# A fused attention and mixture-of-experts kernel: the fourth block's attention moved to the end, expert 0 moved between two blocks

## The reference, cut to what matters

```python
x  = inputs                        # (B=4, S=512, D=128), so 2048 tokens
xn = (x - mean(x)) / sqrt(var(x) + 1e-5)
# attention over each batch row
y = xn @ U                                        # U (128, 32)
attn = softmax(-(n_t + n_j - 2 y_t . y_j))        # n = sum(y*y)
att = attn @ xn
# mixture of 8 experts, two for each token, and a shared expert
xf = xn.reshape(2048, 128)
probs = softmax(rmsnorm(xf) @ router_w.T);  topk_p, topk_i = top_k(probs, 2)
# expert e takes the first 320 of its tokens, in token order
xg = xf[dispatch]                                 # (8, 320, 128)
eout = (silu(xg @ rg) * (xg @ ru)) @ rd           # 8 x (128->512->128)
routed[dispatch] += eout * weight_of_token
shared = (silu(xn @ sg) * (xn @ su)) @ sd         # 128->1024->128
out = x + att + shared + routed
```

## Time and profile before

| what | us |
|---|---|
| median of 3 runs | 156.9 (156.74 to 157.12) |
| the profiled execution, time | 156.88 |
| the profiled execution, span | 155.4 |
| TensorE busy | 150.5 (97% of the span) |
| TensorE weight load busy | 135.1 (87%) |
| VectorE busy | 117.4 (76%) |
| ScalarE busy | 103.5 (67%) |
| GpSimd busy | 83.2 (54%) |

### The profile page before, as it was taken

How to read it: one execution, slowest core, us unless ns; L and a number is a source line. 1 busy time by engine, 2 the same in 40 slices (tenths; PEclk the granted TensorE clock), 3 DMA queues, 4 the chain that set the end, 5 groups by cost and what they waited for, 6 DMA issues and landing times.

```text
span 155.4 us, 3117 instructions
## 1 busy us (share of the span) xinstructions
PE 150.5 (97%) x964; PEld 135.1 (87%) x964; DVE 117.4 (76%) x290; ACT 103.5 (67%) x217; POOL 83.2 (54%) x102
## 2 busy tenths in 40 slices
PE   6999999999999999999999999999999999999992
PEld 6878777889999888888888899999999999878991
DVE  3999969899735599998988777786786786546871
ACT  3369999999469397768756569889677466334100
POOL 7653422357777787877400005698988847454000
PEclk9999999999999999999999999999999999999999
DMA  4999999981111117435069300423232011118486
GB/s 128 302 275 111 210 308 343 343 245 54 55 53 51 51 54 218 158 80 172 0 173 259 124 0 2 152 58 98 67 103 72 25 46 34 30 32 291 96 273 186
DMA packets 26638, 20.72 MB, mean 133 GB/s; under 512 B 2333, under 2 KB 22840, under 8 KB 26624
## 3 DMA queue, kind: packets, MB, share of 16 engines
q1 hardware_dynamic: 24544, 17.76, 42.4%
q0 software_dynamic: 1792, 2.65, 5.6%
q10 hardware_dynamic: 288, 0.14, 0.3%
HBM read 12.36 MB, written 7.92 MB: 131 GB/s over the span
## 4 chain that ended last, share of the span: by engine, by line
PE 92%; DVE 2%; DMA 2%; ACT 1%; POOL 1%; issue 1%; DVEq 0%
PE bank L1259 9%; PE bank L1344 9%; PE bank L1179 8%; PE bank L1181 8%; PE bank L1180 8%; PE bank L1290 8%; PE bank L1284 8%; PE bank L1287 8%; PE bank L1400 5%; PE bank L1402 5%; PE bank L1401 5%; PE bank L1416 2%; PE bank L1244 2%; PE bank L1427 2%; DMA acc<-in_L_attn_x_dram 2%; PE bank L1199 1%
## 5 line engine op out<-in xcount | busy, mean ns | idle before, releaser
L673 ACT ACTIVATE silu<-bank 128x512 f32<-128x512 f32 (+1 forms) x64 | 33.3, 520 | 29.5 <-PE bank L1290 28.9
L567 POOL DMA_INDIRECT slots_dram<-row,slot_i x32 | 34.0, 1063 | 10.9 <-issue 9.4
L1010 DVE TENSOR_TENSOR bank<-bank,silu 128x320 f32<-128x320 f32 (+1 forms) x48 | 27.1, 565 | 15.5 <-ACT silu L673 12.6
L586 POOL DMA_INDIRECT routed_dram<-eo,xg x24 | 23.0, 957 | 11.5 <-DVE eo L1050 6.3
L1016 DVE TENSOR_TENSOR hid_lo<-bank,hid_hi 128x320 fp32r<-128x320 f32 (+1 forms) x48 | 26.2, 546 | 0.0
L681 ACT CAST hid_hi<-bank 128x320 fp32r<-128x320 f32 (+1 forms) x48 | 22.9, 477 | 0.0
L574 POOL TENSOR_TENSOR ew_lo<-sw_raw,ew_hi 128x1024 fp32r<-128x1024 f32 x3 | 7.2, 2414 | 19.3 <-ACT ew_hi L697 19.3
L1010 DVE TENSOR_TENSOR hid_s<-bank,silu 128x512 f32<-128x512 f32 x16 | 11.0, 686 | 5.6 <-PE bank L1181 5.2
L1344 PEld LDWEIGHTS bank<-sd,hid_s 128*128 128x128 f32 x128 | 14.8, 192 | 0.3
L1259 PEld LDWEIGHTS bank<-row,probs 128*128 128x128 f32 x128 | 14.8, 191 | 0.2
L1344 PE MATMUL bank<-sd,hid_s 128*128 128x128 f32 x128 | 15.0, 275 | 0.0
(11 more groups left out here) (204 smaller groups left out, 362.6 us busy)
## 6 DMA issues: line engine op xcount, KB each, us to landing
sw_raw<-in_L_ffn_rg_dram SPq DMA_DIRECT2D x8, 256.0 KB, 3.1
sw_raw<-in_L_ffn_ru_dram SPq DMA_DIRECT2D x8, 256.0 KB, 3.6
rd_raw<-in_L_ffn_rd_dram SPq DMA_DIRECT2D x8, 256.0 KB, 3.4
routed_dram<-fill SPq DMA_DIRECT2D x1, 2048.0 KB, 11.7
routed<-routed_dram SPq DMA_DIRECT2D x8, 256.0 KB, 4.1
slots_dram<-fill SPq DMA_DIRECT2D x1, 1300.0 KB, 12.2
xg<-slots_dram SPq DMA_DIRECT2D x8, 130.0 KB, 2.4
row<-row SPq DMA_DIRECT2D x1, 1024.0 KB, 7.7
```

The costliest lines, as they stand in the source:

```text
L567: G.indirect_dma_start(slots_dram, bass.IndirectOffsetOnAxis(slot_i[:, k, t:t + 1], 0), row[:, t, 0:RW], None, bounds_check=E * CAP - 1, o ...
L673: C.activation(silu[:, q % 2, 0:n], gate_bank(q)[:, 0:n], ACT.Silu).then_inc(silu_ready, 1)
L1010: V.tensor_tensor(hid, up[:, 0:n], silu[:, q % 2, 0:n], ALU.mult).then_inc(hid_ready, 1)
```

## The change

Six edits go together.

- `ORDER` becomes block 0, block 1, expert 0, block 2, experts 1 to 7, block 3.
- Block 3's attention leaves the early stretch. Its `scores` stand between gate and up of the very last chunk, its `exps` are ScalarE's last work (into `end_probs`, which lies in the expert weights' raw buffer), its two `attend` stand inside `down_end_block`, and its two `add_attention` between the two `end_block_sum`.
- The routing puts each token's lower-numbered expert first (`route_in_order`, four small GpSimd operations; `route_swaps`, three; VectorE's `route_order` rewrites `chosen` with 128x256 elements in place of one 128x16 comparison). The 16 indirect DMAs of the lower experts go first, then the other 16. Expert 0 is always the lower of a pair, so its rows are complete after the first 16, and SyncE loads them then.
- `turn_slots(0)` stands behind block 1's chunk 6 and `turn_slots(1)` behind block 2's chunk 6; their `slots_hi` and `slots_lo` in the steps of chunk 7.
- `write_routed(0)` stands ahead of GpSimd's first weight split, which is expert 5's.
- VectorE makes `y_lo(0)` ahead of `route_slots`.

Two down-weight buffers of the second expert move from `yL` and `yR` to the first columns of `xnT_hi` and `xnT_lo`. The diff, cut:

```diff
-    SPREAD = ()
-    ORDER = [("block", b, c) for b in range(EARLY) for c in range(CS)]
-    for e in range(E):
-        ORDER += [("expert", e, c) for c in range(CR)]
-        if e in SPREAD:
-            ORDER.append(("block", B - 1, SPREAD.index(e)))
-    ORDER += [("block", B - 1, c) for c in range(len(SPREAD), CS)]
+    JOBS = [("block", 1), ("expert", 0), ("block", 2)] + [("expert", e) for e in range(1, E)]
+    ORDER = [(*job, c) for job in [("block", 0)] + JOBS + [("block", B - 1)]
+             for c in range(CS if job[0] == "block" else CR)]
     at = {chunk: q for q, chunk in enumerate(ORDER)}
...
 
+        end_score_b = [bank[7], bank[4], bank[5], bank[6]]
+        end_down_b = [bank[0], bank[1]]
...
             for e in range(2, 5):
                 next_expert_weights(e)
                 next_down(e)
-            sp.wait_ge(scattered, 16 * 2 * NT)
-            sp.wait_ge(xg_padded, 1)
-            load_slots(0)
+                if e == 2:
+                    sp.wait_ge(scattered[0], 16 * NT)
+                    sp.wait_ge(xg_padded, 1)
+                    load_slots(0)
+            sp.wait_ge(scattered[1], 16 * NT)
             load_slots(1)
             next_expert_weights(5)
             next_down(5)
...
+            def route_in_order():
+
+                pool.wait_ge(second_ready, 1)
+                after(G.tensor_tensor(behind[:, :], i1, i2, ALU.subtract))
+                after(G.tensor_scalar(behind[:, :], behind[:, :], 0.0, None, ALU.max))
+                G.tensor_tensor(in_order[:, 0, :], i1, behind[:, :], ALU.subtract)
+                G.tensor_tensor(in_order[:, 1, :], i2, behind[:, :], ALU.add).then_inc(order_ready, 1)
+
...
-            G.tensor_scalar(ends[:, :, :], experts[:, :, :], float(CAP), float(CAP), ALU.mult, ALU.add
+            route_in_order()
+            pool.wait_ge(order_ready, 1)
+            G.tensor_scalar(ends[:, :, :], in_order[:, :, :], float(CAP), float(CAP), ALU.mult, ALU.add
                             ).then_inc(ends_ready, 1)
+            route_swaps()
             route_places()
             route_weights()
             pool.wait_ge(slots_emptied, 16)
...
-            for t in range(NT):
-                for k, row in enumerate((row1, row2)):
+            for k, row in enumerate((row1, row2)):
+                for t in range(NT):
                     G.indirect_dma_start(
                         slots_dram, bass.IndirectOffsetOnAxis(slot_i[:, k, t:t + 1], 0), row[:, t, 0:RW], None,
-                        bounds_check=E * CAP - 1, oob_is_err=False).then_inc(scattered, 16)
+                        bounds_check=E * CAP - 1, oob_is_err=False).then_inc(scattered[k], 16)
 
...
+            write_routed(0)
             for e in range(E):
                 if e + EW < E:
                     split_weights(e + EW)
-                write_routed(e)
+                if e > 0:
+                    write_routed(e)
                 if e + RD < E:
                     split_down_weights(e + RD)
...
-                    if j == 0 and b >= 2:
+                    if j == 0 and b == B - 1:
+                        act.wait_ge(ew_split_pool, E - DVE_WEIGHTS)
+                    elif j == 0 and b >= 2:
                         act.wait_ge(att_done, 2 * (b - 1))
...
             act.wait_ge(sd_loaded, 16)
-            exps(3)
...
                         round_down_weights(2)
+                    else:
+                        slots_hi(0)
                 elif kind == "block" and i == EARLY - 1:
                     if c < 2:
...
-                    elif c == 6:
-                        slots_hi(0)
+                    elif c == 7:
+                        slots_hi(1)
                 elif kind == "expert":
-                    if c == 1 and i + 1 < E:
...
             def route_order():
-                V.tensor_tensor(later[:, :], i1, i2, ALU.is_gt).then_inc(later_ready, 1)
+                dve.wait_ge(order_ready, 1)
+                dve.wait_ge(sel_ready, 1)
+                mark(V.tensor_tensor(chosen[:, :, :, :], ids_twice, experts_in_order, ALU.is_equal))
...
             n_lo()
+            y_lo(0)
             route_slots()
-            y_lo(0)
             y_lo(1)
             n_right(1)
...
-            for b in range(1, B):
+            for b in range(1, B - 1):
                 add_attention(b, 0)
                 add_attention(b, 1)
-                if b == B - 2:
-                    dve.wait_ge(sd_hi_s, 1)
-                    V.tensor_tensor(sd_lo, sd[:, :, :], sd_hi.bitcast(F32), ALU.subtract).then_inc(sd_split, 1)
+            dve.wait_ge(sd_hi_s, 1)
+            V.tensor_tensor(sd_lo, sd[:, :, :], sd_hi.bitcast(F32), ALU.subtract).then_inc(sd_split, 1)
             for q in range(FIRST, len(ORDER)):
...
                         split_weights(2, c - 6)
+                        if c == 7:
+                            slots_lo(0)
                 elif kind == "block" and i == EARLY - 1:
...
-                        slots_lo(0)
-                elif kind == "expert" and c == 1 and i + 1 < E:
+                    elif c == 7:
+                        slots_lo(1)
+                elif kind == "expert" and c == 1 and 1 <= i < E - 1:
...
             end_block_sum(0)
+            dve.wait_ge(block_added, B)
+            add_attention(B - 1, 0)
+            add_attention(B - 1, 1)
+            dve.wait_ge(att_added, 2 * B)
             end_block_sum(1)
...
+                elif b == B - 1:
+                    pe.wait_ge(eo_ready, E)
+                    pe.wait_ge(hid_ready, len(ORDER) - 2)
+                    pe.wait_ge(xg_ready, E)
+                    pe.wait_ge(out_copied, len(JOBS))
                 for j in range(TG):
                     if b == 0:
                         pe.wait_ge(hid_ready, CS)
-                    else:
+                    elif b < B - 1:
                         pe.wait_ge(prob_ready, TG * (b - 1) + j + 1)
-                    M(bank[j][:, :], yL[0:NR.stop, S * b + P * j:S * b + P * j + P],
+                    M(score_bank(b, j)[:, :], yL[0:NR.stop, S * b + P * j:S * b + P * j + P],
...
-                if b >= 1:
+                if 1 <= b < B - 1:
                     pe.wait_ge(att_added, 2 * (b - 1) + h + 1)
+                elif b == B - 1:
+                    pe.wait_ge(hid_ready, len(ORDER))
...
-                first, second = turn_b[0], sums_b
-                pe.wait_ge(xg_ready, E)
-                pe.wait_ge(hid_ready, at["block", b, CS - 2])
+                first, second = end_down_b
+                pe.wait_ge(silu_ready, at["block", b, CS - 1])
+                pe.wait_ge(hid_ready, at["block", b, CS - 1])
                 down_tile(first[:, 0:D], 0, range(CS - 2))
-                pe.wait_ge(out_copied, len(JOBS))
                 down_tile(second[:, 0:D], 2, range(CS - 2))
                 pe.wait_ge(hid_ready, at["block", b, CS - 1] + 1)
                 down_tile(first[:, 0:D], 0, range(CS - 2, CS))
                 down_tile(first[:, D:2 * D], 1).then_inc(end_down, 1)
+                attend(b, 0)
+                attend(b, 1)
                 down_tile(second[:, 0:D], 2, range(CS - 2, CS))
                 down_tile(second[:, D:2 * D], 3).then_inc(end_down, 1)
...
             attend(2, 0)
-            scores(3)
             attend(2, 1)
-            attend(3, 0)
-            attend(3, 1)
             for q in range(FIRST, len(ORDER)):
...
+                    elif q == len(ORDER) - 1:
+                        between = lambda: scores(B - 1)
+                    up_of_block(i, c, between)
...
-                if (kind, i, c) == ("block", EARLY - 1, 5):
-                    turn_slots(0)
-                elif kind == "expert" and c == 0 and i + 1 < E:
+                if kind == "block" and i in WIDE and c == CS - 2:
+                    turn_slots(i - 1)
+                elif kind == "expert" and c == 0 and 1 <= i < E - 1:
                     turn_slots(i + 1)
```

More of the change, by code:

```diff
@@ L75, in moe_attention_kernel @@
     LAG = 3
-    JOBS = [("block", b) for b in WIDE] + [("expert", e) for e in range(E)]
     END = at["expert", E - 1, CR - 1]
@@ L147, in moe_attention_kernel @@
         place_i = sb("place_i", [P, 2, NT], I32)
-        later = sb("later", [P, NT])
-        later_i = sb("later_i", [P, NT], I32)
+        behind = sb("behind", [P, NT])
+        swaps = sb("swaps", [P, 3, NT])
+        top_w = sb("top_w", [P, NT])
+        shares = sb("shares", [P, 2, NT])
         slot0_i = sb("slot0_i", [P, E, NT], I32)
@@ L216, in down_weights_of @@
             if s < 2:
[L217 removed]
+                return rd_hi[s], rd_lo[s]
             return rd_more[:, s - 2, 0, :, :], rd_more[:, s - 2, 1, :, :]
@@ L228, in moe_attention_kernel, with probs_of @@
         assert CS == 2 * TG and B % 2 == 0
-        assert CS * D + 2 * CR * D <= T
+        assert CS * D + CR * D <= (B - 1) * S and CR * D <= S
         sd_hi, sd_lo = [t[:, 0:CS * D].rearrange("p (c d) -> p c d", c=CS) for t in (yL, yR)]
```

(11 more changed lines are left out.)

56 lines of the change are left out of this document (37 added, 19 removed).

## The result

The changed kernel took 163.0 us, median of 6 runs (161.71 to 163.85), against 156.95 (156.74 to 157.35) of the kernel before beside it: 1.0381 times as long, 95% interval 1.0331 to 1.043. A later repeat (experiment 10) gave 1.0359 (1.0312 to 1.0406). The direction and both hand-over waits came as forecast; the time lies above the range of 159.3 to 162.2.

What follows compares the result with a forecast made beforehand. The prediction took the kernel as bound by TensorE's list of matmuls plus each place where it waits. 156.88 us before + 0.4 (start) + 1.92 + 1.32 (hand-overs to experts 0 and 1) = 160.5 us; range 159.3 to 162.2.

Steps and rivals of the forecast that it cites:

- both hand-over waits: Last steps of blocks 1 and 2: TensorE waits for VectorE's slot copies, +1.92 us at expert 0, +1.32 at expert 1.
- the spare time of the scatter: Turn of expert 0's rows in block 1: rows there at about 58.4, turn at 60.6, spare 2.2 us, costed at nothing.
- the fall of TensorE's clock: Rival: each of the two waits sets the clock back to half pace, losing 2.05 us each, 164.6; chance 0.04.
- The attention at the end: Block 3's attention, 4.6 us, moves from front to end of TensorE's list; zero, at most 0.5 at block 1.
- The start: Routing before the first scores: longer order chain and VectorE write make `scores(1)` 0.4 us later; bounds 0.1 to 0.7.
- The exchange of `y_lo(0)`: Start of the kernel: `scores(0)` finds its data earlier, but TensorE must soon wait for `scores(1)`; given nothing.
- a rival with a chance of 0.08: Expert 0's rows late: five slow DMAs add 0.2 us, 160.7; a load or wait 1.0 longer, 161.7; chance 0.08.
- the upper bound: Whole kernel: top of the sum's bounds, 160.1 to 161.1 us, without VectorE's 0.5 at block 1.
- the covered hand-overs: Rival, last steps of blocks 1 and 2: copies end within the down matmuls; 156.5 to 157.6, middle 156.9; chance 0.08.

Runs made afterwards that it cites:

- experiment 10: The changed kernel again, five more rounds, no edit: 163.35 us, 1.0359 times the kernel before.
- experiment 5: The changed kernel with block 3's scores, attend and exponentials back in the early stretch: 161.09 us, 1.0269 times the kernel before.
- experiment 8: The kernel before with only the new routing operations, which put the lower expert first: 157.49 us, 1.0017 times the kernel before.
- experiment 1: The changed kernel with the slot copies ahead of chunk 7's silu and product instead of behind: 158.84 us, 1.0103 times the kernel before.
- experiment 9: The changed kernel with one weight split repeated three times ahead of `slots_lo(0)`: 166.95 us, 1.0594 times the kernel before.
- 2: The changed kernel with `y_lo(0)` behind `route_slots` again: 161.34 us, 1.0284 times the kernel before.
- 7: The changed kernel with `turn_slots` behind chunk 5 and the slot copies in chunk 6's step: 161.51 us, 1.0304 times the kernel before.
- 3: The kernel before with only `y_lo(0)` moved ahead of `route_slots`: 158.47 us, 1.0063 times the kernel before.
- 4: The changed kernel with expert 0 behind block 2 again and `write_routed(0)` back in its place: 158.9 us, 1.0086 times the kernel before.
- 6: The changed kernel with slot copies ahead of chunk 7's silu and product, and `y_lo(0)` behind `route_slots`: 158.35 us, 1.0071 times the kernel before.
- 11: The changed kernel with 24 and 16 small matmuls ahead of the gates of experts 0 and 1: 161.79 us, 1.0299 times the kernel before.

## Why the prediction was wrong

Two steps of it failed: the spare time of the scatter, costed at nothing, where the turn then waited 0.92 us; and the fall of TensorE's clock, given a chance of 0.04, which came in 6 of 12 runs and cost 1.3 to 1.9. Beside them the sum took a start, a pace and a time outside the span from the kernel before that the changed kernel did not have, 1.5 us together.

**The hand-overs: right.** Forecast 1.92 and 1.32, measured 1.97 and 1.37; the copy came in the place and after the steps that the sum named. 0.05 more each is a longer way of the semaphore (0.11 from the copy's end to the gate instead of 0.05).

**The attention at the end: right.** No wait there, and experiment 5 shows that taking it back gains nothing but the turn's cover.

**The start: too high.** 0.4 forecast, 0.1 measured, alone as well (experiment 8). Both parts of the term were too long. GpSimd's four steps took 1.15 (27.12 to 28.27) where the sum had 1.41, and VectorE's write took 0.43 and not the 0.60 of `pick`. That the write starts at 28.31, near the 28.1 of the sum, is luck: this trace runs 0.43 late from its first chunk matmul on. The lower bound of 0.1 was the right value. The exchange of `y_lo(0)` does nothing for the scores, as costed.

**The scatter in two halves, "spare 2.2 us: costed at nothing": failed.** The first DMA started at 34.23 (forecast 34.1), so that was right. Three things made the rows later. DMAs 13, 15 and 16 took 1.25, 1.43 and 1.49, and the 16th ended at 55.94 (forecast 54.7): 1.2. SyncE's load followed 2.4 behind it, not 1.15: 1.3. And the turn had its data 3.3 behind the load's issue, not 2.5: 0.8. Together 3.3 against 2.2 spare and 0.2 by which TensorE's list came later to the turn: the measured 0.92. I had the first of the three as a rival with a chance of 0.08 and up to 0.2 us, and the next two only as "a load or a wait 1.0 longer as well".

The 1.15 was read from DMA 32, which lands when little else is moved. DMA 16 now lands beside expert 2's weights. Lines of the list of DMA issues (KB left empty, then us from issue to landing): DMAs 16, 20 and 32 of the kernel before, DMA 16 of the changed kernel, DMA 16 of experiment 5. Then when SyncE issued expert 2's first and last weights in the changed kernel, and the first in experiment 5:

```profile
slots_dram<-row,slot_i POOLq DMA_INDIRECT x1, 2.3
slots_dram<-row,slot_i POOLq DMA_INDIRECT x1, 3.6
slots_dram<-row,slot_i POOLq DMA_INDIRECT x1, 2.1
slots_dram<-row,slot_i POOLq DMA_INDIRECT x1, 3.9
slots_dram<-row,slot_i POOLq DMA_INDIRECT x1, 2.1
```

```profile
53.32 0.33 SPq L386 DMA_DIRECT2D sw_raw<-in_L_ffn_rg_dram  x1
...
55.11 0.38 SPq L390 DMA_DIRECT2D rd_raw<-in_L_ffn_rd_dram  x1
...
57.21 0.33 SPq L386 DMA_DIRECT2D sw_raw<-in_L_ffn_rg_dram  x1
```

Having further DMAs behind it in the queue does not make the landing long: DMA 16 has 16 behind it in all three kernels, and lands 1.3 and 1.1 us behind its own end before and in experiment 5, where no weights are under way (it ends at 54.19 there, the weights come at 57.21). Beside weights it is 2.4 in the changed kernel, and 2.6 for DMA 20 of the kernel before. So the long landing goes with the weights; no edit was made to test that alone, and a few DMAs near 40 us (DMAs 6 and 7 before) land as late without any.

The turn's wait varies: 0 in experiment 1's profile, 0.1 in the repeat's, 1.35 in experiment 9's, with the same scatter and the same place of the turn. What varies is the load: its second part lands 2.0, 2.1 and 3.4 us behind its issue there, and 2.9 in the changed kernel. The larger part of the 3.3 came from the two landings.

The Trainium skill, SBUF — State Buffer, section "Who interferes with whom", has the rule by which I had made the rival: a VectorE instruction with two SBUF inputs contends with a GpSimd instruction that reads SBUF. The trace agrees in part: each of the three slow DMAs has a remainder with both inputs in SBUF beside it, but DMA 19 of the kernel before has such a split beside it for 0.68 us and took 0.97. The same section has `tensor_tensor`, the operation of these remainders, as one that did not stall a DMA; here DMAs beside it took up to 1.49.

**The clock, at a chance of 0.04: failed.** It fell in 2 of 6 runs and in 4 of 6 of the repeat. Its price was forecast as two falls of 2.05, for 164.6; the runs with the fall lie 1.9 above those without in the repeat, and 1.3 to 1.9 in the first six runs and in experiments 2, 5 and 7, about what the sum had for one fall. I had given it that chance since no row of before showed TensorE idle; that was an absence of evidence, and I priced it as if it were evidence against. What the Trainium skill, TensorE: Matmul & The Clock Gate, section "What's actually happening", says of the throttled clock as the state that idleness brings back, the trace now shows inside the kernel (experiment 9, granted 0.50 for 6.7 us). How often runs had a mean clock of 0.989 or less, by the waits that their profiles show:

| kernels | waits of TensorE, us | runs with the fall |
|---|---|---|
| experiments 1, 3, 4, 6 | none, or one of up to 1.4 | 0 of 24 |
| 2 and 5 | 2.0 and 1.4 | 2 of 8 |
| 7 | 3.06 | 2 of 4 |
| the changed kernel, with 10 | 0.1 to 0.9, 2.0, 1.4 | 6 of 12 |
| 11 | as the changed kernel, with 2.4 us of them filled | 0 of 6 |
| 9 | 1.35, 4.15, 1.4 | 4 of 4 |

**What the sum left out.** The sum took the start, the pace and the time outside the span over from the one profiled execution before. The time outside the span is 1.4 to 1.6 before, and 1.7 to 2.1 in the kernels with the whole change, but for one run with 2.9. The pace of 233 ns is worth about 0.4 and goes with the routing operations. The start came 0.43 later, by no edit. For the profiled execution the account closes: 0.92 (the turn) + 0.1 (the hand-overs) - 0.3 (the scores) + 0.43 (the start) + 0.5 (the pace and what is left) + 0.6 (outside the span) = 2.25, which is 162.77 less 160.52. The late rows alone would have stayed within the range, whose upper end had 1.2 for them; with these terms even the four runs without a fall of the clock have a median of 162.6. (Two sums were off by little: the upper bound is 161.2 by its own terms, not 161.1, and the middle of the covered hand-overs, with the start's +0.4, 157.3, not 156.9.)

**What stays open.** Which of the waits lets the clock fall in a given run: the profile caught the fall only in experiment 9. Why the load of expert 0's rows lands up to 1.4 us later in one run than in another. Why the matmuls of 512 columns stand 2 ns further apart with the routing operations. Where the 0.25 to 0.5 outside the span come from.

## What to carry to other kernels

When a job is handed over from one engine to another, count where the hand-over stands in its engine's queue, from the last thing that this queue waits for: here moving two copies ahead of a product took waits of 3.34 us away, and no run with them moved had a lower clock. Price a DMA's landing by a row with the same other transfers under way; that of one which lands when little else moves is too short for one beside weight loads. And a wait on TensorE of some microseconds isn't only its own length: look at the clock of all runs, as the profiled one may be one in which it did not fall.

## What the runs showed of the hardware

In experiment 9 TensorE ran no matmul from 64.46 to 68.44, and the granted clock was 0.50 from 67.7 to 74.4, though 19 matmuls filled all of that from 68.44 on; it cost 2.75 us beside the wait. Filling waits of 2.0 and 1.4 us with small matmuls left no run with a lower clock. At the kernel's start the faster pace comes at a time that differs between executions: in the traces where the small matmuls speed up by 6.2 us the first chunk matmul starts at 8.54 to 8.67, and where they do so at 6.6, 6.8 and 7.0 it starts at 8.88, 8.96 and 9.05. An indirect DMA of 128 rows landed 1.1 to 1.4 us behind its end in most cases, and 2.4 to 2.6 behind it for those named above that ran beside weight loads, wherever it stood in its queue.
